# Projection stage of an attention and expert kernel: transposes one slot earlier and behind the values' matmuls, tokens normalised in two halves, two steps of the scale moved to the vector engine

## What is computed

```python
h = layernorm(x)                                   # per token: (x - mean) / sqrt(var + eps)
q, k = rope(h @ Wq), rope(h @ Wk)                  # 32 heads of 8, rotated by position
v = h @ Wv                                         # 16 heads of 16
x = x + layernorm(differential_attention(q, k, v) @ Wo)
x = x + layernorm(expert_choice_ffn(layernorm(x)))
```

## Time and profile before

| | before |
|---|---|
| runs, device time | 6005.84, 6007.64 and 6008.32 us; median 6007.64 |
| the profiled execution's own time | 6007.5 us |
| its span, first to last instruction | 6005.7 us |
| projection stage, by the timeline | 0 to about 468 us of the span |
| PE busy over the span | 5596.6 us (93%) |
| DVE / ACT / POOL busy over the span | 5494.2 / 4976.1 / 2065.5 us |

### The profile page before, as it was taken

One profiled execution on the slowest core, in us unless ns is written; L12 is line 12 of the kernel. 1 busy time (PEld: TensorE's weight loads), 2 busy tenths in 40 slices (PEclk: granted clock), 3 DMA queues, 4 the chain that ended last, 5 costly groups with the idle time before them and its releaser, 6 DMA issues. The chain is left out here.

```text
span 6005.7 us, 167689 instructions
## 1 busy us (share of the span) xinstructions
PE 5596.6 (93%) x50896; PEld 1965.7 (33%) x50896; DVE 5494.2 (91%) x6072; ACT 4976.1 (83%) x9206; POOL 2065.5 (34%) x3655
## 2 busy tenths in 40 slices
PE   8878999999999999999999999999999999987775
PEld 4541333333333333333333333333333333325423
DVE  7868999999999999999999999999999999957706
ACT  6665999999999999999999999999999999973304
POOL 7981222222222222222222222222222222236406
PEclk9997999999999999999999999999999999998878
DMA  5671222322222223222322232222232222215598
GB/s 178 204 204 50 52 52 52 52 52 52 52 52 52 53 52 52 53 51 51 54 50 52 52 52 51 51 52 51 51 52 52 52 52 52 52 43 194 177 366 270
DMA packets 469606, 495.27 MB, mean 82 GB/s; under 512 B 132051, under 2 KB 330867, under 8 KB 468963
## 3 DMA queue, kind: packets, MB, share of 16 engines
q1 hardware_dynamic: 467939, 485.74, 34.3%
q10 hardware_dynamic: 1024, 0.53, 0.0%
HBM read 360.60 MB, written 123.21 MB: 81 GB/s over the span
## 5 line engine op out<-in xcount | busy, mean ns | idle before, releaser
L741 DVE TENSOR_REDUCE at_largest<-at_ps_m 128x1 f32<-128x1024 f32 x4096 | 4694.1, 1208 | 46.9 <-PE at_ps_m L845 35.2
L707 ACT ACTIVATE at_e<-at_ps_e 128x512 f32<-128x512 f32 x8192 | 4407.7, 598 | 357.7 <-PE at_ps_e L814 157.5
L831 PE MATMUL at_ps_o<-at_e,at_v 128*32 128x256 f32 (+1 forms) x30720 | 2680.4, 421 | 35.2 <-ACT at_e L707 25.3
L845 PE MATMUL at_ps_m<-k_stack,q_stack 48*128 48x512 bf16 x8192 | 2484.8, 384 | 87.9 <-DVE at_largest L741 55.5
L814 PE MATMUL at_ps_e<-q_stack,k_stack 51*128 51x512 bf16 x8192 | 2515.2, 382 | 7.7 <-issue 2.1
L831 PEld LDWEIGHTS at_ps_o<-at_e,at_v 128*32 128x32 f32 x30720 | 844.9, 149 | 1559.5 <-issue 818.4
L814 PEld LDWEIGHTS at_ps_e<-q_stack,k_stack 51*128 51x128 bf16 x8192 | 568.6, 93 | 1665.8 <-ACT at_e L707 1628.2
L626 POOL TENSOR_TENSOR at_negated<-at_zeros,at_largest_t 128x32 f32<-128x32 f32 x256 | 64.7, 253 | 2169.4 <-DVE at_largest_t L748 2169.4
L845 PEld LDWEIGHTS at_ps_m<-k_stack,q_stack 48*128 48x128 bf16 x8192 | 574.7, 93 | 219.5 <-DVE at_largest L741 188.8
L669 POOL TENSOR_TENSOR at_rms<-at_mean_eps,at_minus_half 128x16 f32<-128x16 f32 x128 | 372.6, 2911 | 10.0
L645 POOL TENSOR_TENSOR at_crossed<-at_totals 128x32 f32<-128x32 f32 x128 | 32.2, 252 | 760.9 <-DMA at_totals<-at_sums 760.9
(11 more groups left out here) (132 smaller groups left out, 3003.0 us busy)
## 6 DMA issues: line engine op xcount, KB each, us to landing
k_stack<-k_parts SPq DMA_DIRECT2D x1536, 64.0 KB
q_stack<-q_parts SPq DMA_DIRECT2D x256, 192.0 KB
q_stack<-q_parts SPq DMA_DIRECT2D x256, 128.0 KB
w_first<-in_w SPq DMA_DIRECT2D x32, 1024.0 KB, 11.7
ex_w_second<-in_w SPq DMA_DIRECT2D x32, 1024.0 KB, 12.7
q_parts<-pr_parts SPq DMA_DIRECT2D x96, 256.0 KB, 2.5
k_parts<-pr_parts SPq DMA_DIRECT2D x96, 256.0 KB, 2.8
pr_x_in<-in_x SPq DMA_DIRECT2D x16, 1024.0 KB, 6.0
```

The costliest lines, as they stand in the source:

```text
L707: nc.scalar.activation(e[:, j % E_BUFS], ps_e[:, bank(u, j)], ACT.Exp, scale=SCALE).then_inc(exp_done, 1)
L741: nc.vector.reduce_max(largest[:, u % 2, j // SIDE, j % SIDE:j % SIDE + 1], ps_m[:, j % 2], AX.X).then_inc(max_done, 1)
L831: last = nc.tensor.matmul(ps_o[32 * tile:32 * tile + 32, columns], v[:, u, tile // 2, first:first + 2 * VD * TILES - kt:TILES], e[:, (QUAD ...
L845: last = nc.tensor.matmul(ps_m[:, j % 2, half * HALF:(half + 1) * HALF], q_stack[rows, u, pair, c, t * P:(t + 1) * P], k_stack[rows, u, pa ...
```

## The change

1. PE: the transposes of the next batch go from slots 2 and 3 to slots 1 and 2, and stand behind the values' matmuls of their slot. That is behind slot 1 and behind slot 2, so ahead of the q/k matmuls of slots 2 and 3. Banks 0 and 1 (tokens 0 to 511) wait for the first half of the normalised tokens, banks 2 and 3 for the second half.
2. ACT: `normalise` is split in two halves of four tiles, one at the end of slot 0, one at the end of slot 1, each with a count of `xn_ready` of its own. The copies of banks 0 and 1 stand at the head of slot 2, those of banks 2 and 3 at the head of slot 3.
3. The first and last steps of the scale leave POOL: DVE computes variance + eps and the mean's negative with two small instructions behind the statistics, POOL keeps the power and one multiplication. Tiles `eps` and `zeros` go. Waits that counted `xn_ready` and `pool_step` count in new steps.

```diff
@@ sync: load @@
-                    sp.wait_ge(xn_ready, n - 1)
+                    sp.wait_ge(xn_ready, 2 * (n - 1))
@@ gpsimd: scale @@
                     pool.wait_ge(var_done, m + 1)
-                    nc.gpsimd.tensor_tensor(var[:], mean_var[:, :, 1], eps[:], ALU.add).then_inc(pool_step, 1)
-                    pool.wait_ge(pool_step, 3 * m + 1)
                     if not (isinstance(m, int) and m == 0):
-                        pool.wait_ge(xn_ready, m)
+                        pool.sem_inc(pool_passed, 1)
+                        pool.wait_ge(xn_ready, 2 * m)
                     nc.gpsimd.tensor_tensor(rstd[:], var[:], minus_half[:], ALU.pow).then_inc(pool_step, 1)
-                    pool.wait_ge(pool_step, 3 * m + 2)
-                    nc.gpsimd.tensor_tensor(shift[:], mean_var[:, :, 0], rstd[:], ALU.mult).then_inc(pool_step, 1)
-                    pool.wait_ge(pool_step, 3 * m + 3)
-                    nc.gpsimd.tensor_tensor(bias[:], zeros[:], shift[:], ALU.subtract).then_inc(rstd_done, 1)
+                    pool.wait_ge(pool_step, m + 1)
+                    nc.gpsimd.tensor_tensor(bias[:], neg_mean[:], rstd[:], ALU.mult).then_inc(rstd_done, 1)
@@ scalar: normalise, slot @@
-                def normalise(m, u):
+                def normalise(m, u, side):
                     act.wait_ge(rstd_done, m + 1)
                     if not (isinstance(m, int) and m == 0):
-                        act.wait_ge(t_done, TILES // 2 * m)
-                    for t in range(TILES):
+                        act.wait_ge(t_done, KC * (2 * m - 1 + side))
+                    for t in range(side * TILES // 2, (side + 1) * TILES // 2):
...
-                    if ch == 3 and more:
-                        for j in range(4):
+                    if ch >= 2 and more:
+                        for j in range(2 * (ch - 2), 2 * (ch - 1)):
                             copy_transposed(n + 1, 1 - u, j)
...
-                    if ch == 0 and more:
-                        normalise(n + 1, 1 - u)
+                    if ch < 2 and more:
+                        normalise(n + 1, 1 - u, ch)
@@ vector: statistics @@
-                    last.then_inc(var_done, 1)
+                    last.then_inc(dve_step, 1)
+                    dve.wait_ge(dve_step, 2 * m + 2)
+                    nc.vector.tensor_scalar(neg_mean[:], mean_var[:, :, 0], -1.0, None, ALU.mult)
+                    nc.vector.tensor_scalar(var[:], mean_var[:, :, 1], EPS, None, ALU.add).then_inc(var_done, 1)
@@ tensor: transposes, slot @@
                 def transposes(m, banks):
-                    pe.wait_ge(xn_ready, m + 1)
                     for j in banks:
+                        if j % KC == 0:
+                            pe.wait_ge(xn_ready, 2 * m + j // KC + 1)
                         pe.wait_ge(t_copied, 4 * m + j - 1 + 2)
...
-                    if ch >= 2 and more:
-                        transposes(n + 1, (0, 1) if ch == 2 else (2, 3))
                     pe.wait_ge(v_copied, c - 1 + 2)
...
                     last.then_inc(v_done, 1)
+                    if ch in (1, 2) and more:
+                        transposes(n + 1, (0, 1) if ch == 1 else (2, 3))
```

More of the change, by code:

```diff
@@ L125, in project @@
             w = sb("w", [P, KC, 3, D])
-            eps, minus_half, zeros = sb("eps", [P, TILES]), sb("minus_half", [P, TILES]), sb("zeros", [P, TILES])
+            minus_half = sb("minus_half", [P, TILES])
             x_in = sb("x_in", [P, 2, TILES, D])
@@ L129, in project @@
             var, rstd = sb("var", [P, TILES]), sb("rstd", [P, TILES])
-            shift, bias = sb("shift", [P, TILES]), sb("bias", [P, TILES])
+            neg_mean, bias = sb("neg_mean", [P, TILES]), sb("bias", [P, TILES])
             xn = sb("xn", [P, TILES, D])
@@ L151, in project @@
             v_stored = [sem("v_stored0"), sem("v_stored1")]
-            dve_step, pool_step, passed = sem("dve_step"), sem("pool_step"), sem("passed")
+            dve_step, pool_step, passed, pool_passed = sem("dve_step"), sem("pool_step"), sem("passed"), sem("pool_passed")
             x = io["x"].rearrange("b (t p) d -> b p t d", p=P)
@@ L240, in _ @@
             def _(pool):
-                nc.gpsimd.memset(eps[:], EPS).then_inc(pool_set, 1)
                 nc.gpsimd.memset(minus_half[:], -0.5).then_inc(pool_set, 1)
-                nc.gpsimd.memset(zeros[:], 0.0).then_inc(pool_set, 1)
                 nc.gpsimd.memset(ones[:], 1.0).then_inc(ones_set, 1)
-                pool.wait_ge(pool_set, 3)
+                pool.wait_ge(pool_set, 1)
                 pool.wait_ge(ones_set, 1)
@@ L350, in drain @@
                     second_part(c - 1, (c - 1) % RING)
-                normalise(0, 0)
+                for side in range(2):
+                    normalise(0, 0, side)
                 for j in range(4):
@@ L370, in statistics @@
                     last.then_inc(dve_step, 1)
-                    dve.wait_ge(dve_step, m + 1)
+                    dve.wait_ge(dve_step, 2 * m + 1)
                     if not (isinstance(m, int) and m == 0):
```

## The result

| | before | changed |
|---|---|---|
| median of the runs | 6007.64 us (5 runs, 6005.84 to 6011.19) | 6044.75 us (5 runs, 6031.91 to 6050.07) |
| ratio | | 1.0060, 95% interval 1.0049 to 1.0072 |
| profiled execution | 6007.5 us, span 6005.7 | 6044.75 us, span 6042.9 |
| attention stage begins at | 468.5 us | 508.3 us |
| from there to the end | 5537.2 us | 5534.6 us |

The change costs 0.6%: 37.1 us by the medians, 37.2 by the two spans. So those 2.6 us say nothing of the change.

What follows compares the result with a forecast made beforehand. The prediction took a DVE and POOL chain as the bound, closed through slot 2's matmuls after the change; 28.8 + 0 + 1 + 7 = +37 on 6007.5 us gave 6044 us, range 6022 to 6064.

Steps and rivals of the forecast that it cites:

- the closed chain through slot 2's matmuls: Loop over the engines: leave_out(0) would wait for slot 2's matmuls, behind transposes that wait for ACT; period 28.21 us.
- start and batch 0: Before the loop's steady periods: first tokens ready up to 2.0 us earlier, batch 0 pays 0 to 2.4; net 0.
- 12 periods, order and scale: The loop's 12 periods, each 2.40 us longer from the transposes' new order and the scale's move: +28.8 us.
- 12 periods, clock: PE's clock falling behind the new gap in one batch of three, 4 x 1.7 us: +7, between 0 and 38.
- tail: Last three batches: 7.2 us longer, less 6.2 as ACT's two waits for stores shrink by 3.1 each; net +1.
- What bounds: The claim that a DVE and POOL chain sets the 25.81 us period and PE's 2.95 us of waits lie off it.
- Segment B: From the aggregation's end through POOL's scale to add(2)'s end: 5.75 us, to become 6.04, 0.29 longer.
- Segment C: DVE and POOL from third(0), behind add(2), to third(2)'s end: to stay 13.22 us.
- Segment D: From third(2)'s end to leave_out(0)'s end: 3.38 us, to become 5.49, 2.11 longer, as transposes hold slot 2's matmuls.
- the rival with 0.20: The clock falls in every batch, 12 x 1.7 = 20 us in place of 7: 6057 us, chance 0.20.
- Rows 9 and 10: Profile rows of PE's gaps and clock: 0.50 behind 6.60 us, slow transposes behind 4.84, clock 1.07 behind 2.68.
- The rival on the other side: Faster: PE's waits of 2.95 us a batch go, 12 x 2.95 = 35 us less, 5972 us; chance 0.08.

Runs made afterwards that it cites:

- PE kept busy: The changed kernel with 32 transposes of the identity added on PE behind slot 1's values, ahead of the wait for the first half: 6037.1 us, ratio 1.0047.
- the put-back version: The changed kernel with its transposes put back ahead of the values' matmuls of slots 2 and 3, the rest kept: 6006.6 us, ratio 0.9996.
- the transposes one slot later: The changed kernel with transposes behind the values' matmuls in slots 2 and 3, all four copies at slot 3's head: 6016.1 us, ratio 1.0012.

## Why the prediction was right, point by point

6044 was forecast, 6044.75 measured, inside the range. The structure held: the period is the closed chain through slot 2's matmuls, which accounts for 27.1 of the 37 us. One term was wrong, the clock's, and the total is as close as it is by luck. The terms, with batch 1's and batch 13's q matmuls as marks (before 46.41 and 356.26, changed 46.23 and 393.12, PE kept busy 45.15 and 382.14):

| term | forecast | measured |
|---|---|---|
| start and batch 0 | 0 | 46.23 - 46.41 = -0.2 |
| 12 periods, order and scale | +28.8 | 336.99 - 309.85 = +27.1 (PE kept busy) |
| 12 periods, clock | +7 | 346.89 - 336.99 = +9.9 |
| tail | +1 | 115.2 - 112.3 = +2.9 |
| the stages behind | 0 | -2.6 |

- **What bounds.** That PE's waits cost nothing while they stand behind slot 2's matmuls is shown by the put-back version, where leave_out(0) waits 2.02 us for POOL with slot 2's products done.
- **Segment B** was forecast 0.29 longer and is 0.16: the two small steps and the wait put leave_out(1) 2.47 behind the aggregation, not 2.60. They add 0.32, just under the forecast's lower bound of 0.35. That add(2) would run into it holds (3.27).
- **Segment C** 13.17 against 13.22.
- **Segment D** was forecast 5.49. With the clock up it is 5.51, with third(3) unblocked and leave_out(0) stopped by it, as worked out. B, C and D together are 0.16 under the forecast, which is the period's 28.05 against 28.21. The gap behind slot 1, forecast 4.4, is 4.5 with the clock up and 4.34 without.
- **The clock** is the term that was mis-sized, in two ways that nearly cancel. "A fall in one batch of three" was wrong: it fell in every batch from the second on, which was the rival with 0.20. "I take 1.7" a fall was wrong too: with falls the period is 0.4 or 1.5 over 28.05, 1.0 in the mean, since half of them end sooner and the slack at leave_out(0) takes part of each. 4 falls of 1.7, 7 us, stand against 11 falls of 0.9, 9.9 us. The bound of 0.4 to 3.2 a fall held. The rival's own sum, 6057, had the falls right and their price twice too high. That the total is right to a microsecond is luck: clock and tail came 4.8 us above the forecast, order, start and the stages behind 4.5 below it.
- **Rows 9 and 10** were read as if a gap's length decided. The later rows say it does not alone: 3.14 in batch 1 of the changed kernel left the clock up, 3.16 in the same place did not when it was run again, nor did 2.60 elsewhere. What else decides stays open; behind 4.3 us and more in the loop it fell each time.
- **The tail**: both waits for stores are still there, 3.98 and 8.66 us, where 6.75 and 8.94 less 3.1 each were expected. The first shrank as forecast, the second didn't.
- **The rival on the other side** needed the tokens 3.0 us sooner; the wait of 4.34 shows they were not. Its sum, PE's idle time times the batches, took a busy engine for the bound.

## What to carry to other kernels

In a loop over several engines follow one period from end to end before crediting a wait: a wait of a nearly full engine can be worth nothing, and the order of two blocks on that engine can close a longer loop through all the others. When an instruction moves ahead of another, ask whether what it waits for is there at the new place, and who waits for the one that it now holds up. A step moved to an engine that shares a port is priced by what runs on the other side at that moment and by what stands behind it, not by its own 0.17 us.

## What the runs showed of the hardware that was not expected

- A DVE scalar operation on 8 elements a partition waits for POOL's running instruction: 1.07 us at the median in one order, 0.85 in another, 0.17 where POOL is idle. The Trainium skill, SBUF — State Buffer, section "Who interferes with whom", names `tensor_scalar` among the operations that can take the shared ports; the trace agrees, for 8 elements too. In the changed kernel POOL was always idle there, so the forecast lost nothing by leaving it out.
- The clock's falls are a cost that repeats with the loop: periods of 28.45 and 29.58 by turns, in two executions. And a wait that nothing depends on can start one, as with the transposes one slot later (25.96 against 27.65).
- Filling a 4.34 us gap of PE with 3.66 us of transposes that nobody needs took 1.0 us off the period.
